# Mean embedding and projection: a shorter order for the first mean, the bias buffers as a sixth raw weight block, and ScalarE moving all products until tile 2's join

## What is computed

```python
valid = sequence_ids < emb_table.shape[0]
seq_emb = emb_table[where(valid, sequence_ids, 0)] * valid[..., None]
user_repr = seq_emb.sum(axis=1) / maximum(valid.sum(axis=1, keepdims=True), 1.0)
logits = user_repr @ proj_w + proj_b          # (1024, 512) @ (512, 12500) + (12500,)
```

## Time and profile before

| | |
|---|---|
| median of three runs | 638.0 us |
| profiled execution | 639.96 us |
| its span, first to last instruction | 638.1 us |
| mean granted TensorE clock | 0.997 |
| TensorE busy | 609.2 us (95%) |
| VectorE busy | 407.6 us (64%) |
| GpSimd busy | 231.1 us (36%) |
| ScalarE busy | 145.6 us (23%) |
| ScalarE, high half of a block, mean | 1875 ns (39 of them) |
| ScalarE, move of a bank, mean | 587 ns (38 of them) |
| TensorE, five columns of tile 0 in a row, from 40.96 us | 4.61 us |

### The profile page before, as it was taken

How to read it: one execution, slowest core, us unless ns; L and a number is a source line. 1 busy time by engine, 2 the same in 40 slices (tenths; PEclk the granted TensorE clock), 3 DMA queues, 4 the chain that set the end, 5 groups by cost and what they waited for, 6 DMA issues and landing times.

```text
span 638.1 us, 7597 instructions
## 1 busy us (share of the span) xinstructions
PE 609.2 (95%) x2602; PEld 477.3 (75%) x2602; DVE 407.6 (64%) x723; ACT 145.6 (23%) x161; POOL 231.1 (36%) x227
## 2 busy tenths in 40 slices
PE   1989889989999999999999999999999999999997
PEld 0337558768788787788888888888888888888886
DVE  7988949899878898697885554332333333344442
ACT  8917425132122131300200221111011111211210
POOL 5777877777763767566550000000000000000000
PEclk9998999999999999999999999999999999999999
DMA  9979999999997999798893398454555555566632
GB/s 310 387 257 342 385 394 344 358 303 324 315 302 267 311 302 315 238 325 248 253 339 114 99 293 283 123 168 163 173 167 174 177 178 177 175 191 202 218 127 103
DMA packets 77704, 158.31 MB, mean 248 GB/s; under 512 B 9288, under 2 KB 65043, under 8 KB 77659
## 3 DMA queue, kind: packets, MB, share of 16 engines
q1 hardware_dynamic: 60378, 110.30, 51.1%
q0 software_dynamic: 17280, 47.47, 22.9%
HBM read 115.70 MB, written 51.20 MB: 262 GB/s over the span
## 4 chain that ended last, share of the span: by engine, by line
PE 72%; DVE 19%; issue 5%; DMA 2%; DVEq 1%; ACT 0%; POOL 0%; POOLq 0%
PE acc L842 70%; DVE sums L561 7%; DVE w_lo L625 5%; DMA rows<-in_L_rec_emb_table_dram,index 2%; DVE key L518 1%; DVE top L514 1%; DVE stage L640 1%; PE acc L847 1%; DVEq L259 1%; DVE index L516 0%; PE turned L763 0%; PE turned L783 0%; DVE mean L607 0%; DMA ids_sb<-in_r_sequence_ids_dram 0%; DVE key L502 0%
## 5 line engine op out<-in xcount | busy, mean ns | idle before, releaser
L353 POOL DMA_INDIRECT rows<-in_L_rec_emb_table_dram,index x208 | 221.6, 1066 | 96.3 <-issue 55.8
L842 PE MATMUL acc<-w_hi,mean_hi 128*128 128x500 f32 x800 | 225.3, 403 | 0.8 <-ACT mean_hi L438 0.8
L640 DVE TENSOR_TENSOR stage<-acc,bias_sb 128x500 f32<-128x500 f32 x162 | 109.3, 676 | 179.2 <-PE acc L842 179.1
L842 PE MATMUL acc<-w_lo,mean_hi 128*128 128x500 f32 x800 | 214.6, 390 | 0.0
L842 PE MATMUL acc<-w_hi,mean_lo 128*128 128x500 f32 x800 | 213.7, 389 | 0.4 <-DVE mean_lo L612 0.3
L842 PEld LDWEIGHTS acc<-w_hi,mean_hi 128*128 128x128 f32 x800 | 150.7, 190 | 32.0 <-issue 4.3
L842 PEld LDWEIGHTS acc<-w_lo,mean_hi 128*128 128x128 f32 x800 | 150.8, 189 | 31.5
L842 PEld LDWEIGHTS acc<-w_hi,mean_lo 128*128 128x128 f32 x800 | 150.3, 188 | 32.1 <-DVE mean_lo L612 1.2
L561 DVE SCALAR_TENSOR_TENSOR sums<-rows,mask,sums 128x512 f32<-128x512 f32 x165 | 124.0, 752 | 16.2 <-issue 8.2
L422 ACT ACTIVATE w_hi<-w_raw 128x2000 fp32r<-128x2000 f32 x39 | 72.9, 1875 | 235.3 <-PE acc L842 215.8
L625 DVE TENSOR_TENSOR w_lo<-w_raw,w_hi 128x1000 fp32r<-128x1000 f32 x74 | 85.3, 1194 | 13.6 <-ACT w_hi L422 13.6
(11 more groups left out here) (106 smaller groups left out, 193.1 us busy)
## 6 DMA issues: line engine op xcount, KB each, us to landing
out_dram<-stage SPq DMA_DIRECT2D x200, 250.0 KB, 3.9
w_raw<-in_L_rec_proj_w_dram SPq DMA_DIRECT2D x39, 1000.0 KB, 6.6
bias_sb<-in_L_rec_proj_b_dram SPq DMA_DIRECT2D x39, 250.0 KB, 4.9
raw_at_hi<-in_L_rec_proj_w_dram SPq DMA_DIRECT2D x4, 1000.0 KB, 11.6
rows<-in_L_rec_emb_table_dram,index POOLq DMA_INDIRECT x208, 6.0
raw_at_lo<-in_L_rec_proj_w_dram SPq DMA_DIRECT2D x3, 1000.0 KB, 15.2
stage<-in_L_rec_proj_w_dram SPq DMA_DIRECT2D x1, 1000.0 KB, 26.1
ids_sb<-in_r_sequence_ids_dram SPq DMA_DIRECT2D x1, 700.0 KB, 4.4
```

The source lines that it names most:

```text
L353: return pool.indirect_dma_start(out=dst, out_offset=None, in_=table, in_offset=bass.IndirectOffsetOnAxis(ap=column, axis=0), bounds_check ...
L640: dve.tensor_tensor(stage[:, g % STAGE, r - stores[g][0]], acc[:, r % BANKS, 0:BW], bias_sb[:, i % BIAS], ALU.add).then_inc(s_moved_by_dve, 1)
L842: last = nc.tensor.matmul(bank, first, second, start=part + k == 0, stop=part == 2 and k == K - 1 and not by_act[r])
```

## The change

- VectorE's product for tile 0's share of further rows (`first_further_share`) is taken out of `first_mean` and stands right behind `sum_further(0)`, ahead of low half 3. Of the sort of tile 2 only two rounds stay ahead of the first mean; three go behind its low part.
- TensorE sums tile 0's rest ahead of column 14 and lists tile 1's ahead of column 17.
- The four bias buffers together serve once as a raw buffer, for block 5. The buffers of later blocks shift: block 6 goes where block 0 was, 7 where 1 was, and so on. `LATE_LOAD` becomes block 8. SyncE loads the first four bias blocks at unit 16, when low half 5 is made.
- ScalarE moves all units until tile 2's join (`ACT_TILES` 2): units 11, 13, 15, 17, 19 and 21 change from VectorE to ScalarE. From unit 22 on, nothing changes in who moves.

```diff
     RAW_MORE, MORE_LOADS = 2, 16
-    FURTHER_BEHIND, LIST_FIRST_AT, BIAS_DUE = 20, 21, 3
-    ACT_TILES, BOTH_TILES = 1, 5
+    SORTED_FIRST = 2
+    FURTHER_BEHIND, LIST_FIRST_AT = 20, 17
+    ACT_TILES, BOTH_TILES = 2, 5
...
-    LATE_LOAD, REST_FIRST_AT, OPENED = 7, 18, SPLIT - 1
+    LATE_LOAD, REST_FIRST_AT, OPENED = 8, 14, SPLIT - 1
...
     ONCE = RAW + RAW_MORE
-    raw_slot = [q if q <= ONCE else (q - 1) % ONCE if q < MORE_LOADS else q % RAW for q in range(LOADS)]
+    IN_BIAS = ONCE + 1
+    raw_slot = [q if q <= IN_BIAS else (q - 2) % ONCE if q < MORE_LOADS else q % RAW for q in range(LOADS)]
...
-        s_raw = [sem(f"w_loaded{i}") for i in range(RAW + RAW_MORE + 1)]
+        s_raw = [sem(f"w_loaded{i}") for i in range(IN_BIAS + 1)]
...
                 return raw_once
+            if raw_slot[q] == IN_BIAS:
+                return bias_sb[:]
...
             for r in range(UNITS):
-                if r == BIAS_DUE:
+                if r == joined[ACT_TILES] - 6:
+                    sp.wait_ge(s_w_lo, IN_BIAS + 1)
                     for i in range(BIAS):
                         load_bias(i)
...
+            def first_further_share():
+
+                dve.tensor_scalar(rest_mean[:], sums[:], inv_count[:, 0:1], None, ALU.mult).then_inc(s_further_mean, 1)
+
             def first_mean():
 
-                dve.tensor_scalar(rest_mean[:], sums[:], inv_count[:, 0:1], None, ALU.mult).then_inc(s_further_mean, 1)
...
             sum_further(0)
+            first_further_share()
             w_low(3)
-            for r in range(ROUNDS):
+            for r in range(SORTED_FIRST):
                 sort(2, r)
             first_mean()
             mean_low(0)
+            for r in range(SORTED_FIRST, ROUNDS):
+                sort(2, r)
```

More of the change, by code:

```diff
@@ L105, in mean_embedding_projection @@
     assert MORE_LOADS < JOIN[TILES // 2] and RAW_AT + BW <= (STAGE - K) * BW
+    assert BIAS == K
     split_due = [None] * SPLIT + [min(last_unit[q - SPLIT] + 1, first_unit[q] - 1) for q in range(SPLIT, LOADS)]
```

## The result

The changed kernel takes 646.62 us (median of 4 runs, 642.50 to 647.49) against 638.08 for the kernel before on the same chip: ratio 1.0118, 95% interval 1.0084 to 1.0152. The ratios in this document are estimates over all runs and not quotients of two medians. By this one the kernel is slower by 7.5 us (the two medians lie 8.5 apart); forecast were 636.2 us and a chance of 0.10 for slower. The profiled execution took 647.49 us, span 645.7, so it reads 0.9 us above the median. All later ratios are against runs of the kernel before on the same chip (medians 638.5 to 639.1).

What follows compares the result with a forecast made beforehand. TensorE's row of products and the waits inside it were taken to set the end. Terms: 0 + 0 - 1.3 - 0.5 = -1.8 us, giving 636.2 us for the median (638.2 profiled); range 634.5 to 638.4.

Steps and rivals of the forecast that it cites:

- Part 2: Bias buffers as a block: four bias broadcasts and 1000 KB leave the busiest stretch and come at unit 16; priced 0.
- Part 1: The shorter order of the first mean: unit 8 starts when GpSimd's chain of gathers lets it; priced 0.
- upper bound of 1.4: First mean 1.4 us late if tile 0's column 25 takes 6.2 us to land; bounds -0.7 to +1.4, taken +0.9.
- VectorE's lateness is covered: Tile 1: VectorE runs 3.4 us late up to the last add, against a slack of 4.2 at column 24's gather.
- Tile 2's column 2: Its gather needs column 17's buffer: slack 2.4, so 1.0 us late, a cost for tile 2, not for unit 8.
- Phases, 0 +- 0.8: Low halves and gathers meeting in SBUF may fall in other phases: 0.8 us in all, either sign, taken as 0.
- Part 3: ScalarE's six more moves: 1.3 us gained by tile 2's join, 0.5 at tile 3's, bias products included.
- (c): Block 7's weights slow tile 0's last gathers, mean 3.3 late, VectorE past its slack: 639.2 us; chance 0.11.
- (a): Joins of tiles 2 and 3 don't give; bias products eat most of the gain: about 637.3 us; chance 0.26.
- (b): Less traffic lands tile 1's column 25 in 4.5 us instead of 6.0, moving unit 8: 634.7 us; chance 0.13.
- (d): The first mean is no earlier; this was the forecast itself, priced at 0, hidden by the wait at 86.47.
- signs named ahead: Wrong if unit 8 starts over 1 us from 87.0, VectorE's adds release tile 1's gathers, or tile 2's turn waits over 1 us.

Runs made afterwards that it cites:

- experiment 10: The kernel of experiment 5 with the bias transfers at unit 7 instead of unit 16: 637.45 us, 0.9978 of the kernel before.
- 7: The mended kernel with block 7 held until tile 0's last gather landed and all five sorting rounds ahead of the first mean: 636.55 us, 0.9967.
- experiment 8: The kernel before with ScalarE's moves, the earlier share and TensorE's earlier rest and list, five sorting rounds ahead of the mean: 637.0 us, 0.9975.
- experiments 1: The changed kernel with block 15 put into the raw buffer that block 12 used instead of block 14's: 640.07 us, 1.0017 of the kernel before.
- experiment 2: The kernel before with only block 15 put into block 14's raw buffer, so block 17 waits for low half 15: 645.77 us, 1.0111.
- experiment 5: The mended kernel with all five sorting rounds of tile 2 ahead of the first mean: 637.14 us, 0.9971 of the kernel before.
- experiment 12: The mended kernel with the same three sorting rounds placed behind the add of tile 1's column 13: 639.52 us, 1.0015 of the kernel before.
- experiment 4: The kernel before with only ScalarE moving all units until tile 2's join: 637.2 us, 0.9972.
- experiment 3: The kernel before with only the first mean's order changed: earlier share, rest and list, three sorting rounds behind the mean: 640.58 us, 1.0032.
- experiment 9: The changed kernel with all five sorting rounds ahead of the first mean, block 15's buffer left as changed: 644.21 us, 1.0092 of the kernel before.
- the mended kernel: The changed kernel with block 15's buffer put back, three sorting rounds still behind the mean: 640.07 us, 1.0017 of the kernel before.

## Why the prediction was wrong

The step that failed by its size is **Part 2, "bias buffers as a block: 0"**. It priced the bias transfers and the traffic, and both were right (experiment 10, and 7 against 8). It never followed what a sixth block in rotation does to the blocks behind it. The shift carries through to block 15, where the rule of the buffers changes, and load 17 has to wait for low half 15 instead of 14 and goes out 29 us later. That costs 6.5 to 7 us (experiments 1 and 2): a wait of 5.35 us of the weight loads at tile 3's turn where 1.14 was forecast to halve, and 2.1 us at half clock behind it. No rival held it, and neither did the range.

**Part 1, order of the first mean: 0.** The mean was 1.5 us late, just past the upper bound of 1.4; column 25 landed after 6.1 us, which is the case that bound was made from. That the early order itself gives nothing was right (experiment 8). Wrong was that VectorE's lateness is covered. Its adds came 3.9 us later (65.10 against 61.22) instead of 3.4, and the slack was looked up at column 24 and at tile 2's column 2 only. It was also taken 0.9 us too large there, the time that passes between an add's end and the gather it frees; column 24's 4.2 were really 3.3, less than the delay of 3.4. Column 16's were fewer: add of column 5 done at 61.97, 0.9 to the gather, 62.9; issued at 65.97; 3.1 us. Tile 2's column 0 had 2.2 and column 2 had 1.5. With the gathers ahead falling otherwise column 16's slack is smaller still, since experiment 5 has that gather at 64.79. In time the three rounds cost 2.9 us, most of it at unit 8 (88.60 against 86.02), the rest at tile 2. Tile 2's column 2, forecast 1.0 late "for tile 2, not for unit 8", waited 0.7 beyond its usual 0.3.

**Phases, 0 +- 0.8.** They did move unit 8 by about this much: experiment 12 has column 25's gather at 78.81 and experiment 5 at 79.96, from one slow gather fewer. The pairing itself held. The Trainium skill, "SBUF — State Buffer", Who interferes with whom, infers that such a tensor_tensor leaves descriptor generation alone; the runs disagree once more, as the last section shows.

**Part 3, ScalarE's moves: -1.8.** Right in size and place: 1.8 us in experiment 4, the wait for tile 2's mean gone, unit 21 1.8 and unit 34 2.3 earlier. Tile 2's turn came at 128.37 rather than 129.3 there, 0.6 of it because unit 8 was earlier too.

**The sum** as measured: 6.5 for the hand-over, 2.9 for the rounds, -1.8 for the moves, and 0 for the early order and the bias transfers: +7.6 against 7.5 measured. That these meet says little, since the first two are differences between neighbouring kernels on the way from the changed one to experiment 5, and must add up. Each edit put alone into the kernel before gives 7.1 (experiment 2), 2.0 (experiment 3, by another road) and -1.8 (experiment 4), +7.3 together. The prediction had -1.8 alone.

**Rivals.** (c) was the nearest in kind, a late mean with VectorE past its slack, but by another road: the mean was 1.5 late, not 3.3, and weights did not starve the gathers. Tile 0's last gather landed in 6.1 us and tile 2's last two in 7.1 and 6.4, with loads queued. The Trainium skill, "DMA: Bandwidth & Descriptors", Queues, rings and completion order, with its turns packet by packet, fits that, so (c)'s own mechanism did not occur. (a) and (b) were not the case. (d), that the mean is no earlier, was so. Of the signs named ahead, unit 8 was 1.2 off, which I had called wrong, and a gather released by VectorE's adds was there.

Open: why experiment 9 gave back only 1.7 us by the ratios where its trace gave 3.8. Of the 2.1 between, 1.3 is that the one profiled execution lay 0.9 above its median and the other 0.4 below. Open too is why one run of the changed kernel came out at 642.5 us with a mean clock of 1.0 while the other three stood at 0.991 to 0.994. A turn without half clock behind it would explain 2.1 of its 4.5 us; no trace of that run exists.

## What to carry to other kernels

When a buffer joins a rotation, write out the whole table, which load waits for which reader, old beside new, and look above all at the place where the rule changes: one entry cost more here than everything else. Then ask when, in time, the new predecessor is done, for one block later meant 29 us here. When an engine that frees buffers gets later, the slack (with the 0.9 us from release to gather taken off) to compare is the smallest over all gathers that reuse one, in order, not that of the one nearest the wait; moving the work further back moves the wait to the next pair. Two edits of one change can be right on their own: here the moves alone gave 0.9972, and the mended kernel with five rounds ahead and the later load gave 0.9967, the lowest time found, if not clear of the moves alone. And a unit start read from one trace is worth little below the spread of equal code, here 1.5 us at unit 8.

## What the runs showed of the hardware that was not expected

**A gather beside a low half.** In experiment 5 the low half of block 10 and a gather share their time (VectorE, GpSimd):

```profile
76.48 2.30 DVE L635 TENSOR_TENSOR w_lo<-w_raw,w_hi 128x1000 fp32r<-128x1000 f32 x2
```

```profile
77.72 1.94 POOL L360 DMA_INDIRECT rows<-in_L_rec_emb_table_dram,index  x1 [0.30 <-issue]
```

In experiment 12, with sorting rounds in that place and the low half moved to 79.08, the same gather, column 24's, (77.51) took 0.99. This 0.95 us is about what unit 8 is earlier by than in experiment 5 (85.04 against 86.02). Not every gather beside a low half is slow: the next one, at 78.81, runs into the low half of 79.08 and takes 1.00.

**The clock after a short wait.** In the trace of the kernel before TensorE's first unit ran at half clock. It ran at full clock after the change, and also in experiment 2, whose kernel is the one before until block 15 is loaded. Windows 48 to 52 us of before, of after, and of experiment 2:

```profile
48.00:52.00 4.00, 3.50 (x9) 2.90 (x10) 2.87 (x5) 2.12 (x2) 3.00 (x3) 0.57 1.05 401
```

```profile
48.00:52.00 4.00, 2.67 (x13) 2.14 (x14) 2.52 (x10) 2.36 (x2) 3.00 (x3) 1.00 0.97 359
```

```profile
48.00:52.00 4.00, 3.47 (x15) 2.76 (x16) 2.86 (x4) 2.15 (x2) 3.00 (x3) 1.00 1.03 396
```

So unit 0 lasted 4.33, 2.84 and 2.83 us, after waits of the weight loads for the mean of 2.32, 1.77 and 2.27 us. The same code after nearly the same wait got either clock, so the length of this wait does not decide it, and these rows don't tell what does. It is also by this luck alone that a mean 1.5 us late cost nothing at unit 1 in the table: against experiment 2's trace the changed kernel is 1.5 us late at unit 1 and 2.8 at unit 8.
